# B of the two VectorE-made scan inputs: by DMA through the shared ring instead of spread by TensorE into PSUM

## What is computed

```
dA     = exp(dt[t, i] * A[i, n])                    # decay
state  = dA * state + dt[t, i] * B[t, n] * u[t, i]  # scan, one per state n
y[t,i] = sum over n of state[i, n] * C[t, n]        # product and sum
```

## Time and profile before

| | |
|---|---|
| time, median of 3 runs | 966.35 us (964.02 to 968.66) |
| span of the profiled execution | 963.9 us |
| median of the runs less that span | 2.45 us |
| TensorE busy | 846.2 us (88%), 2178 matmul records |
| VectorE busy | 839.9 us (87%) |
| GpSimd busy | 819.0 us (85%) |
| ScalarE busy | 585.7 us (61%) |
| DMA queue of SP | 257.79 MB, 77.4% of 16 engines' span |

### The profile page before, as it was taken

How to read it: one execution, slowest core, us unless ns; L and a number is a source line. 1 busy time by engine, 2 the same in 40 slices (tenths; PEclk the granted TensorE clock), 3 DMA queues, 4 the chain that set the end, 5 groups by cost and what they waited for, 6 DMA issues and landing times.

```text
span 963.9 us, 8874 instructions
## 1 busy us (share of the span) xinstructions
PE 846.2 (88%) x2178; PEld 363.3 (38%) x2178; DVE 839.9 (87%) x632; ACT 585.7 (61%) x798; POOL 819.0 (85%) x374
## 2 busy tenths in 40 slices
PE   5688989989898899989989898998989889898776
PEld 2233433334443334334343333333443333433322
DVE  2489999888999988998998999999899989889991
ACT  3575765848476583855758486574857657484331
POOL 0598997979989797997989799898989979798990
PEclk9799999989999998989999999999999999899997
DMA  1699688978778798778869788896988779689760
GB/s 46 222 295 305 244 274 285 315 261 281 262 291 303 260 313 293 260 252 288 314 255 318 266 282 258 306 312 253 309 283 280 262 285 325 244 301 302 263 247 3
DMA packets 78051, 258.35 MB, mean 268 GB/s; under 512 B 13104, under 2 KB 15408, under 8 KB 78000
## 3 DMA queue, kind: packets, MB, share of 16 engines
q1 hardware_dynamic: 78000, 257.79, 77.4%
HBM read 254.60 MB, written 3.15 MB: 267 GB/s over the span
## 4 chain that ended last, share of the span: by engine, by line
POOL 51%; DMA 17%; issue 17%; PE 6%; DVE 5%; ACT 3%; SPq 1%; POOLq 1%; DVEq 0%; ACTq 0%
POOL inp L881 31%; POOL state L887 17%; DMA b_all<-bc_dram 14%; DMA c_all<-bc_dram 3%; POOL du L871 3%; DVE ps_x L1031 2%; PE ps_y L546 1%; DVE state L1031 1%; PE ps_w L459 1%; DVE state L1038 1%; ACT ps_x L730 1%; PE ps_x L531 1%; SPq L308 0%; PE ps_w L507 0%; POOL step L873 0%
## 5 line engine op out<-in xcount | busy, mean ns | idle before, releaser
L881 POOL TENSOR_TENSOR inp<-du,b_all 128x1024 f32<-128x1024 f32 x224 | 521.9, 2354 | 4.9 <-DMA b_all<-bc_dram 4.0
L546 PE MATMUL ps_y<-state,packed 128*128 128x512 f32 x1024 | 495.6, 623 | 19.5 <-POOL state L887 19.5
L1031 DVE TENSOR_TENSOR_SCAN ps_x<-ps_x,inp 128x1024 f32<-128x1024 f32 x144 | 329.3, 2287 | 42.5 <-ACT ps_x L730 29.8
L887 POOL TENSOR_TENSOR state<-state,c_all 128x1024 f32<-128x1024 f32 x112 | 262.0, 2351 | 87.0 <-DVE state L1024 49.4
L730 ACT ACTIVATE ps_x<-step,a_neg 128x1024 f32<-128x1024 f32 x224 | 247.1, 1112 | 137.7 <-DVE state L1038 101.0
L546 PEld LDWEIGHTS ps_y<-state,packed 128*128 128x128 f32 x1024 | 194.2, 197 | 267.5 <-issue 213.0
L1038 DVE TENSOR_TENSOR state<-ps_x,c_all 128x1024 f32<-128x1024 f32 x144 | 175.9, 1222 | 4.2 <-issue 0.7
L1031 DVE TENSOR_TENSOR_SCAN state<-ps_x,inp 128x1024 f32<-128x1024 f32 x80 | 179.1, 2272 | 0.0
L531 PE MATMUL ps_x<-u,w_b_wide 128*128 128x512 f32 x128 | 68.0, 656 | 9.4 <-DVE state L1038 9.3
L1024 DVE TENSOR_TENSOR_SCAN state<-decay,ps_x 128x1024 f32<-128x1024 f32 x32 | 73.0, 2281 | 0.5
L459 PE MATMUL ps_w<-xpad,w_conv 128*128 128x512 f32 x128 | 61.6, 605 | 3.3 <-ACT xpad L692 3.3
(11 more groups left out here) (116 smaller groups left out, 676.4 us busy)
## 6 DMA issues: line engine op xcount, KB each, us to landing
c_all<-bc_dram SPq DMA_DIRECT2D x256, 512.0 KB, 6.8
b_all<-bc_dram SPq DMA_DIRECT2D x224, 512.0 KB, 6.0
xt<-in_x_t SPq DMA_DIRECT2D x32, 64.0 KB, 3.3
bc_dram<-bc_rows SPq DMA_DIRECT2D x32, 64.0 KB, 3.2
out<-ofin SPq DMA_DIRECT2D x16, 64.0 KB, 1.6
packed<-in_packed SPq DMA_DIRECT2D x1, 635.0 KB, 4.2
packed<-in_packed SPq DMA_DIRECT2D x1, 129.0 KB, 2.1
w_qkv<-in_w_qkv SPq DMA_DIRECT2D x1, 64.0 KB, 2.2
```

The lines of the kernel that those rows point to most:

```text
L546: last = mm(ps_y[:, HALF * half:HALF * (half + 1)], ident, state[n % H_RING][:, HALF * half:HALF * (half + 1)], start=(n == 0), stop=(n == ...
L881: tt(inp[i % IN_RING][:, :], du[b.buf][:, :], b_all[i % B_RING][:, :], ALU.mult).then_inc(pool_inputs, 1)
L887: tt(state[n % H_RING][:, :], state[n % H_RING][:, :], c_all[n % C_RING][:, :], ALU.mult).then_inc(pool_products, 1)
L1031: v.tensor_tensor_scan(held if KIND[n] == "P" else x, x, inp[i % IN_RING][:, :], 0.0, ALU.mult, ALU.add).then_inc(scans, 1)
```

## The change

B of states 0 and 4 is loaded like that of the others. The ring b_all now takes all 16 states of an image in their order, so the tile of state n is b_all[n % 4], and its load waits until the input of state n - 4 has been made, by whichever engine makes it (`input_wait`). SP's list gets load_b of states 0 and 4, and some of the others change places. `spread_b`, the weight w_b_wide, its two setup copies and the semaphore b_spread go. VectorE's `scan_input` multiplies du and the loaded tile, both in SBUF, and writes to ps_x as before; the wait for a free ps_x moves from TensorE to it.

```diff
+        def input_wait(b, n):
+
+            if n < 0:
+                b, n = b + -1, n + N
+            if KIND[n] == "D":
+                return dve_inputs, dve_in_index(b, n) + 1
+            return pool_inputs, pool_in_index(b, n) + 1
+
...
                 all_at_least(sp, (bc_rows_done, j.num + 1), (pool_inputs, NPI * (j.num - 1)),
-                             (pool_products, NPO * (j.num - 1)), (dve_products, NDO * (j.num - 1)))
+                             (dve_inputs, NDI * (j.num - 1)), (pool_products, NPO * (j.num - 1)), (dve_products, NDO * (j.num - 1)))
...
             def load_b(b, n):
 
-                i = pool_in_index(b, n)
-                all_at_least(sp, (bc_stored, 32 * (b.num + 1)), (pool_inputs, i - B_RING + 1))
+                i = N * b.num + n
+                all_at_least(sp, (bc_stored, 32 * (b.num + 1)), input_wait(b, n - B_RING))
                 sp.dma_start(b_all[i % B_RING][:, :], bc_dram[b.buf][n, :].partition_broadcast(128)
                              ).then_inc(b_loaded[i % B_RING], 16)
...
                 store_bc(first)
+                load_b(first, 0)
                 load_b(first, 1)
                 load_b(first, 2)
                 load_b(first, 3)
-                load_b(first, 5)
                 load_c(first, 0)
                 load_c(first, 1)
                 load_c(first, 2)
-                load_b(first, 6)
+                load_b(first, 4)
+                load_b(first, 5)
                 load_c(first, 3)
...
             def steps(b, done, coming, later):
+                load_b(b, 6)
                 load_b(b, 7)
                 load_b(b, 8)
                 if later:
...
                 load_c(b, 14)
                 if coming:
+                    load_b(coming, 0)
                     load_b(coming, 1)
                 if done:
                     store_out(done)
...
                     load_b(coming, 2)
                     load_b(coming, 3)
-                    load_b(coming, 5)
                     load_c(coming, 0)
                     load_c(coming, 1)
                     load_c(coming, 2)
-                    load_b(coming, 6)
+                    load_b(coming, 4)
+                    load_b(coming, 5)
                     load_c(coming, 3)
...
-            def spread_b(b, n):
-
-                pe.wait_ge(u_done, 2 * (b.num + 1))
-                if b.num == 0 and n % 2 == 1:
-                    pe.wait_ge(x2_done, 2)
-                at_least(pe, *x_free_wait(b, n - 2))
-                for half in range(2):
-                    last = mm(ps_x[n % 2][:, HALF * half:HALF * (half + 1)], w_b_wide[:, BY_DVE_IN.index(n), :],
-                              u[b.buf][:, HALF * half:HALF * (half + 1)], start=True, stop=True)
-                last.then_inc(b_spread, 1)
...
-                spread_b(b, 4)
...
-                if coming:
-                    spread_b(coming, 0)
...
             def scan_input(b, n):
                 i = pool_in_index(b, n)
                 pool.wait_ge(du_done, b.num + 1)
-                pool.wait_ge(b_loaded[i % B_RING], 16 * (i // B_RING + 1))
+                pool.wait_ge(b_loaded[n % B_RING], 16 * ((N // B_RING) * b.num + n // B_RING + 1))
                 at_least(pool, scans, scan_count(BY_POOL_IN, NPI, i - IN_RING))
-                tt(inp[i % IN_RING][:, :], du[b.buf][:, :], b_all[i % B_RING][:, :], ALU.mult
+                tt(inp[i % IN_RING][:, :], du[b.buf][:, :], b_all[n % B_RING][:, :], ALU.mult
                    ).then_inc(pool_inputs, 1)
...
             def scan_input(b, n):
 
-                dve.wait_ge(b_spread, dve_in_index(b, n) + 1)
+                dve.wait_ge(b_loaded[n % B_RING], 16 * ((N // B_RING) * b.num + n // B_RING + 1))
                 dve.wait_ge(du_done, b.num + 1)
-                v.tensor_tensor(ps_x[n % 2][:, :], du[b.buf][:, :], ps_x[n % 2][:, :], ALU.mult
+                at_least(dve, *x_free_wait(b, n - 2))
+                v.tensor_tensor(ps_x[n % 2][:, :], du[b.buf][:, :], b_all[n % B_RING][:, :], ALU.mult
                                 ).then_inc(dve_inputs, 1)
```

More of the change, by code:

```diff
@@ L104, in build @@
         w_step = sb("w_step", [I, I])
-        w_b_wide = sb("w_b_wide", [I, NDI, 128])
         wf4 = sb("wf4", [128, 1])
@@ L207, in build @@
         sb_decay_done = sem("sb_decay_done")
-        b_spread = sem("b_spread")
         pool_inputs = sem("pool_inputs")
@@ L569, in prologue @@
                 bc_proj(first)
-                spread_b(first, 0)
                 qkv(second)
@@ L700, in conv_silu @@
                     at_least(act, du_done, j.num - 1)
-                    at_least(act, b_spread, NDI * (j.num - 1))
                 f(u[j.buf][:, HALF * half:HALF * (half + 1)], ps_w[:, HALF * half:HALF * (half + 1)], ACT.Silu,
@@ L965, in setup @@
                 v.tensor_scalar(w_mean[:, :], w("ident2"), -1.0 / C, wf4[:, :], ALU.add, ALU.mult)
-                for k, n in enumerate(BY_DVE_IN):
-                    at = START["w_bc"] + n
-                    v.tensor_copy(w_b_wide[:, k, :], packed[:, at:at + 1].broadcast_to([I, 128]))
                 dve.wait_ge(a_exp_done, 1)
```

## The result

The changed kernel takes 1072.97 us (median of 4 runs, 1068.91 to 1074.01) against 965.18 (963.15 to 968.66) for the kernel before, run beside it: a ratio of 1.110, 95% interval 1.107 to 1.114. That is slower, as forecast, but 64 us more than the forecast and 28 beyond the range.

A forecast was written before the change was run, and what follows sets the result against it. VectorE's order was taken to make the period of some 56 us. 54.4 - 12.7 - 3 + 4.0 = +42.7 gave a span of 1006.6; with the 2.45 offset, 1009 us, range 975 to 1045.

The forecast's parts named there:

- wait of B8, C5 and product 5: SP's queue: B8 issued 5.3 us later, so C5 delays VectorE's product 5; 3.4 us an image, +54.4.
- GpSimd's waits for C: One B less ahead of C0 shortens GpSimd's waits for C tiles, and VectorE's for GpSimd: -3, between 0 and -12.6.
- two SBUF operands: VectorE's inputs 0 and 4 read du and b_all from SBUF: 0 to 6 us more, taken as 0.
- spread gone, start: VectorE's waits for TensorE's spread B go, -12.7; the first image's input 0 waits for B0, +4.0 once.
- TensorE without the spread: TensorE loses 128 matmul records, 68.0 us; nothing counted beyond VectorE's 12.7 us of waits for them.
- The main term: The later B8 on SP's ordered queue and the loads behind it: +54.4 us, 43 to 67 with other C5 times.
- Of the 3.9, the wait of 0.53 at scan 8 vanishes: VectorE: product 5 is 3.9 us late, but scan 8's decay wait of 0.53 goes, leaving 3.4 an image.
- Small waits for decays: VectorE's waits for ScalarE's decays, read from the list of waits as small.
- rival (a): GpSimd holds off VectorE's two-SBUF-operand inputs 0 and 4: +18, 1027 us with the short wait, chance 0.27.
- The long wait of rival (a): GpSimd's back-to-back inputs hold off VectorE's input 4 until GpSimd starves for B8: +2.8 an image, 1064 us, chance 0.08.
- TensorE's time is worth what waited for it: Removing TensorE's spreads gains only VectorE's 12.7 us of waits for them at line 1014.
- GpSimd's path: Late B8 delays GpSimd's input 8 by 1.8 to 2.5 us; through product 3 and softplus, scan 8 by 0.4 to 1.1.

The follow-up runs named there:

- the wait alone: Kernel before, plus one wait: SP waits for VectorE's input 4 ahead of loading B8; 1035.01 us, ratio 1.075.
- spreads kept: Changed kernel with both spreads still made by TensorE into ps_x and waited for by VectorE, then overwritten; 1050.54 us, ratio 1.088.
- one PSUM operand: Changed kernel with VectorE multiplying du by what lies in ps_x instead of the loaded B; 1037.17 us, ratio 1.075.
- the ring of eight: Changed kernel with eight tiles in the ring of B instead of four; 973.05 us, ratio 1.009.
- tiles of their own: Kernel before with B of states 0 and 4 loaded into two separate tiles, no spreads, ring and B8's wait as before; 982.37 us, ratio 1.021.
- C loaded first: Changed kernel with C4, C5 and C6 issued ahead of B8 in SP's list; 1063.05 us, ratio 1.105.
- that path cut too: Changed kernel with C4, C5, C6 ahead of B8 and TensorE's step projection ahead of the sum of state 3; 1045.27 us, ratio 1.084.

## Why the prediction was off

The direction and the place were right. The size wasn't: the span was to grow by 42.7 us and grew by 107.6. By the terms of the sum:

| term | predicted | measured | from |
|---|---|---|---|
| wait of B8, C5 and product 5 | +54.4 | +71 alone; +69.6 with the scans in the changed kernel | the wait alone; products +93.8, scans -24.2 |
| GpSimd's waits for C | -3 | in the line above | |
| two SBUF operands | 0 | +28.3 busy | inputs by line |
| spread gone, start | -12.7 + 4.0 | -8.7 | inputs' waits |
| TensorE without the spread | 0 | +17.3 | norm's wait, spreads kept |

**Right.** B8 leaves 0.08 us after input 4. C5 lands 10.2 us after B8 leaves, 10.3 predicted. The spread waits are gone. The start cost 4.6 instead of 4.0 (scan 1 of the first image starts at 47.04, not 42.40 as in the earlier trace rows).

**The main term, mis-sized by 16 us.** "Of the 3.9, the wait of 0.53 at scan 8 vanishes" failed. ScalarE in image 7 of after:

```profile
514.94 1.28 ACT L723 ACT_TABLE_LOAD   x1 [5.83 <-DVE state L1029]
516.23 1.12 ACT L723 ACTIVATE ps_x<-step,a_neg 128x1024 f32<-128x1024 f32 x1
517.37 1.28 ACT L705 ACT_TABLE_LOAD   x1
518.66 1.11 ACT L708 ACTIVATE step<-ps_w,packed 128x1024 f32<-128x1024 f32 x1
```

Ahead of decay 7 stands a table load that also waits for product 5, so softplus starts at 518.66, 3.8 after product 5's end and not the 2.4 that I allowed; scan 8 is 3.65 behind it, at 522.31, with the old 0.53. That is 0.53 x 16 = 8.5 us. The trace of the kernel before had it already: product 5 ends at 461.03, this load follows, and softplus starts 3.8 later, at 464.84.

```profile
461.11 1.28 ACT L730 ACT_TABLE_LOAD   x1
```

"Small waits for decays" was a wrong reading as well: they are 29.8 us, the largest of VectorE's waits.

The other 8 are C5: late by 3.9 in image 7 as predicted, but 69.6 / 16 = 4.4 on average.

**The hold, taken as nothing.** I had it as rival (a), 18 us at 0.27, and put it at nothing in the sum, since "the rate per element is the same in every VectorE row of this shape"; but those rows have an operand in PSUM. The two kernels with one operand changed settle it: in the kernel before two SBUF operands cost 20 us, in the changed kernel taking them away gives 36 back. The rule of the Trainium skill (page "SBUF — State Buffer", section "Who interferes with whom") was borne out: the one that comes second is held until the first has ended; input 4 ends 1.09 us behind the GpSimd instruction in each of the 16 images. The long wait of rival (a), in which GpSimd's row of inputs keeps the way shut, didn't happen. Image 7 of the changed kernel can't tell, as input 4 meets the last input of the row there; but with the spreads kept it got in at the next boundary amid the row (1.67 us), and so it did in image 8 of the changed kernel (1.66). The price of the hold was neither of the two of rival (a): it hangs on where in GpSimd's instruction VectorE arrives.

**The spread's time, valued at what waited for it.** "TensorE's time is worth what waited for it" missed that the spread of state 4 and that of state 0 also kept TensorE busy and its queue full. Without them it stops for 2.9 us ahead of the output projection and works at 0.60 behind it; the norm comes 1 us late; input 4 meets GpSimd's boundary from the wrong side; and B8 waits for input 4. Three runs act on that chain: the spreads kept put the norm and the hold back (-22), one PSUM operand takes the hold out (-36), the ring of eight takes B8 off the chain (-100). The three overlap, so they don't add up to 108. The first link holds for the changed kernel alone: with tiles of their own and no spreads the norm waited 8.8 us in all. What else has to come together there stays open.

**GpSimd's path, under-priced.** It cost nothing extra in the changed kernel, where it lies beside that of C5, but alone it costs nearly the same: with C loaded first only 10 us came back, and with that path cut too, C7 and C11 took over. The step that failed is the passage from GpSimd's late product to softplus, taken at TensorE's full rate: behind the stop TensorE works at half its clock.

Still open: why C5 comes later in most images than in image 7, and which of the two spreads keeps the norm on time; they were only kept together. Of the kernels tried, none that computes the whole is faster than the one before.

## What to carry to other kernels

A load's wait in an in-order issue queue is a wait of everything behind it: before a ring is shared, compare when the new releaser ends with when the old one did, then follow all tiles behind that load, on every engine that takes them (one such wait, put into the kernel before, cost 71 us, and in the changed kernel a deeper ring took 100 of 108 away). Work taken off an engine isn't a gain if the engine then waits for its next input; what stood beside the removed work has to be looked at as well. And a term that no row shows, but for which a mechanism speaks, belongs in the sum at its worked-out price, not at nothing.

## What the runs showed of the hardware

- An instruction of VectorE with two SBUF operands, held off by a GpSimd instruction, shows the hold in its own duration and not as idle time: 1.2 us becomes up to 3.45, with a median of 1.8 over the 32 of the changed kernel. With a PSUM operand it is 1.20 to 1.23.
- GpSimd pays too: its five inputs of image 7 took 11.68 us in the changed kernel, where input 4 met only the last of them, and 12.60 with the spreads kept, where input 4 (488.89 to 490.56) fell amid them (480.16 to 492.76). With two SBUF operands in the kernel before, its six inputs took 14.92 instead of 13.93.
- TensorE's clock fell behind many of its stops. After a stop of 2.7 us the same four spread records took 3.74 us at a granted clock of 0.51 (the level of 1.2 GHz), and 1.88 at 1.00 (2.4 GHz) where they had matmuls right ahead of them in the kernel before. The length of the stop alone doesn't tell: in image 7 of the kernel with a PSUM operand at the ring of four, a stop of 3.1 us ahead of the output projection was followed by a granted clock of 1.00.
